# Cross-attention, first batch: another share-out of work between VectorE, ScalarE and GpSimd ahead of and in the first softmax

## The chip, the core and the metric

The kernel runs on one core of one Trainium2 chip. The metric is device time in microseconds for one execution; lower is better. TensorE (PE) multiplies matrices, VectorE (DVE), ScalarE (ACT) and GpSimd (POOL) do elementwise work, and SyncE (SP) issues the DMAs. The engines run their own instruction streams and wait for each other on semaphores. Each stream is in order: an instruction that waits holds back all that stand behind it.

## What is computed

Two layers on `x` [8, 512, 512]. The change touches only the first, a cross-attention with a gate:

```python
def _L0_xattn_ref(encoder_hc, decoder_hq, w_sim, b_sim, W_qv, b_qv):
    w1, w2, w3 = (w_sim[:d], w_sim[d:2 * d], w_sim[2 * d:])
    Sim = (encoder_hc @ w1)[:, :, None] + (decoder_hq @ w2)[:, None, :] \
        + jnp.einsum('bid,bjd->bij', encoder_hc * w3, decoder_hq) + b_sim[0]
    A = jax.nn.softmax(Sim, axis=2)
    hq_hat = jnp.einsum('bij,bjd->bid', A, decoder_hq)
    Batt = jax.nn.softmax(jnp.max(Sim, axis=2), axis=1)
    hc_bar = jnp.einsum('bi,bid->bd', Batt, encoder_hc)[:, None, :]
    hc_hat = jnp.broadcast_to(hc_bar, encoder_hc.shape)
    feats = jnp.concatenate([encoder_hc, hq_hat, encoder_hc * hq_hat, encoder_hc * hc_hat], axis=-1)
    return feats @ W_qv + b_qv

x = x + jnp.tanh(g_xattn[0]) * _L0_xattn_ref(_layernorm(x, axis=-1), ctx_1024, ...)
x = x + jnp.tanh(g_ffn[0]) * _L0_ffn_ref(_layernorm(x, axis=-1), ...)   # expert attention, unchanged
```

`encoder_hc` is the normalised `x` of a batch (512 rows of 512), `decoder_hq` its context.

## The kernel before

All is float32. To multiply at fp32 accuracy, each operand is kept as a pair: the upper part, which ScalarE makes by a copy into fp32r, and the lower part, operand less upper part, which VectorE or GpSimd makes (`take_lo`, L229 of both engines). Each product takes three passes over such pairs, so a 128 x 512 result over 512 inner rows is 12 matmuls.

The cross-attention runs over 8 batches. A batch is 4 tiles of 128 rows, and what is transposed is 4 tiles of 128 columns. For each batch:

- front: VectorE normalises `x` (`stage`; statistics L526, then the inverse square root by Newton steps in `mean_rstd`, L46 to L70, 17 small operations, then L537), TensorE turns it (L800), ScalarE copies it into `e_t` (L407). VectorE takes the dot of every row with `w1` (`row_dot`, L545, into `ew1`, then `+ b_sim`, L568) and makes `es_t` (scaled `e_t`, L557, and its lower part). ScalarE and VectorE or GpSimd split the transposed context `c_t` and the context `c`.
- softmax, one tile of 128 rows after another: 12 matmuls into `ps_s`, row maximum on VectorE (L594), `exp` on ScalarE (L435, with its sum), reciprocal and division on VectorE (L599, L601), turn on TensorE (L822), upper part on ScalarE (L440), lower part on VectorE (L606).
- attended: 4 x 12 matmuls into `ps_h` with the small softmax over rows between them (`ps_b`; `mtot` L613, `pmax` L617, `gmax` L677), `h_t` and `eh_t` as pairs (GpSimd makes the lower part of `eh_t`), and the weight block `wec = w_e + hc * w_c` as a pair (L715, L481, L229).
- features: 36 matmuls for each tile into `ps_f` with the weights `wh`, `weh`, `wec`; then the residual (L729), for which GpSimd has added the bias row to `x_sb` (L381). TensorE turns the next batch's rows between them, and has the last features of one batch between the scores of the next.

The loop over batches 1 to 7 is the same code for all; batch 0 has an order of its own written out (`first_front`, `first_softmax`, the head of GpSimd's stream), since the weights arrive and are split then too. Buffers are shared at the start: `x_sb` holds the first transposed context until batch 0's residual is loaded into it; `weh_raw` and `wh_raw` (in `spare`) hold the first context and a weight block, then the other blocks. SP's queue loads in order, each load waiting until its buffer is free: batch 1's `x` (L268, waits for the turn and the dot of each tile), the residual (L292), `weh_raw` behind `c_lo`, `we_raw` behind four `w_lo`, `wc_raw` behind eight.

In batch 0, TensorE turns batch 1's four tiles among the features, and these two waits tie that to GpSimd. ScalarE (L479 to L487), in `attended`:

```python
for k in range(ND):
    act.wait_ge(wec_ready, b * ND + k + 1)
    act.activation(wec[:, 0, k, :], tmp[:, k, :], ACT.Copy).then_inc(wec_hi, 1)
    if more and k in (1, 2):
        if k == 1:
            act.wait_ge(hc_ready, b * ND + ND)
            act.wait_ge(et_lo, b * ND + ND)
        copy_e(b + 1, k - 1)
```

and TensorE (L796 to L798), in `turn_e`: from the third tile on it waits for ScalarE's copy of the tile two before.

```python
if t >= 2:
    pe.wait_ge(et_copied, b * NT + t - 1)
```

## Time and profile before

| | us |
|---|---|
| median of 3 runs | 1286.59 |
| lowest and highest | 1286.2 and 1287.35 |
| the profiled execution | 1285.23 |
| its span from first to last instruction | 1283.4 |

| engine | busy us | share of the span |
|---|---|---|
| TensorE | 1216.2 | 95% |
| VectorE | 846.1 | 66% |
| GpSimd | 668.5 | 52% |
| ScalarE | 644.2 | 50% |

The granted clock of TensorE was 0.983 of full on average. Read first whose busy share is near the whole, then where in time that engine stands and for whom. The profile has views for that: windows (busy time of each engine in a stretch), waits (who waited for whom), the timeline (instructions in order of time, neighbours of one kind merged) and a view by line or tile. In the timeline a row is: start in us, duration in us, engine, line, operation, output <- inputs, shape, count, and in brackets how long the engine had stood before and who released it. The durations of TensorE's matmuls overlap a little.

### The profile page before, as it was taken

To read this page: it belongs to the slowest core of one execution; us is meant where nothing else is said; L and a number is where in the kernel's file an instruction comes from. 1 tells how busy PE (TensorE), PEld (TensorE's weight loads), DVE (VectorE), ACT (ScalarE), POOL (GpSimd) and SP (SyncE) were. 2 spreads that over 40 slices of the span, in tenths; PEclk is the share of its full clock that TensorE was granted. 3 is DMA by queue.
4 is the path that set the end of the run, shared out by engine and by line. 5 is a ranking of instruction groups with operands and counts; after the bars stand their busy time and mean duration, and the time that the engine had idled before them with its cause. 6 is when DMAs were issued, how large, how long until landed. Compare 5 with 4: busy or idle time off the path is not lost.

```text
span 1283.4 us, 19763 instructions
## 1 busy us (share of the span) xinstructions
PE 1216.2 (95%) x6376; PEld 910.7 (71%) x6376; DVE 846.1 (66%) x1527; ACT 644.2 (50%) x1418; POOL 668.5 (52%) x487
## 2 busy tenths in 40 slices
PE   3799999999999999699999999999999999999995
PEld 2588888888888888576767667667767667677663
DVE  7777777777776846264675665675665755756655
ACT  3343434344343431366566566556556656665551
POOL 4543342424242433339397395595593692872972
PEclk9799999999999999799999999999999999999998
DMA  6231313141323213400002002001010010010010
GB/s 215 96 115 50 114 49 123 41 123 41 123 68 96 91 55 134 136 1 13 22 2 98 1 16 82 0 33 65 0 65 33 0 65 33 0 65 0 8 57 33
DMA packets 40714, 75.74 MB, mean 59 GB/s; under 512 B 3760, under 2 KB 4272, under 8 KB 40688
## 3 DMA queue, kind: packets, MB, share of 16 engines
q1 hardware_dynamic: 40688, 75.42, 17.8%
q8 instruction: 13, 0.21, 0.1%
q14 instruction: 13, 0.11, 0.0%
HBM read 58.63 MB, written 16.78 MB: 59 GB/s over the span
## 4 chain that ended last, share of the span: by engine, by line
PE 48%; DVE 5%; POOL 3%; ACT 1%; issue 1%; DVEq 0%; POOLq 0%; ACTq 0%
PE ps_r L1651 11%; PE ps_o L1724 8%; PE ps_s L1711 8%; PE ps_s L1703 7%; PE ps_r L1663 5%; PE ps_r L1686 5%; DVE z L1438 2%; POOL v_acc L1243 2%; DVE z_tmp L1427 1%; POOL spare L1237 1%; PE ps_r L1677 1%; PE ps_r L1670 1%; PE ps_r L1640 1%; DVE nmax L1407 1%; DVE q L1465 0%
## 5 line engine op out<-in xcount | busy, mean ns | idle before, releaser
L1255 POOL TENSOR_TENSOR z<-z,z_tmp 128x1280 f32<-128x1280 f32 x40 | 117.2, 2929 | 199.6 <-DVE z_tmp L1427 197.5
L1407 DVE TENSOR_REDUCE nmax<-ps_s 128x1 f32<-128x512 f32 x256 | 163.6, 680 | 85.7 <-PE ps_s L1703 84.6
L1303 ACT ACTIVATE pt<-ps_s 128x512 f32<-128x512 f32 x256 | 139.2, 595 | 144.5 <-PE ps_s L1711 144.2
L1294 ACT ACTIVATE probs<-ps_s,nmax 128x512 f32<-128x512 f32 x256 | 174.3, 694 | 16.0 <-DVE nmax L1407 15.9
L1243 POOL TENSOR_TENSOR v_acc<-v_acc,spare 128x512 f32<-128x512 f32 x128 | 172.7, 1349 | 10.0
L1237 POOL TENSOR_TENSOR spare<-xv,pick 128x512 f32<-128x512 f32 x128 | 142.5, 1113 | 10.0
L1711 PEld LDWEIGHTS ps_s<-ident,probs 128*128 128x128 f32 x1024 | 109.5, 141 | 48.7 <-issue 40.8
L1711 PE MATMUL ps_s<-ident,probs 128*128 128x128 f32 x1024 | 140.3, 280 | 1.3 <-ACT probs L1294 1.2
L1703 PE MATMUL ps_s<-k,q 64*128 64x512 f32 x768 | 123.6, 426 | 3.7 <-ACT pt L1303 3.7
L1724 PE MATMUL ps_o<-pt,v_acc 128*64 128x512 f32 x512 | 116.9, 598 | 0.7 <-ACT pt L1303 0.7
L229 POOL TENSOR_TENSOR e_t<-e_t 128x512 fp32r<-128x512 f32 x32 | 40.7, 1311 | 146.9 <-ACT e_t L428 146.9
L1703 PEld LDWEIGHTS ps_s<-k,q 64*128 64x128 f32 x768 | 62.3, 184 | 55.8 <-issue 47.3
L788 PE MATMUL ps_h<-es_t,c 128*128 128x512 f32 x384 | 99.0, 408 | 0.0
L788 PE MATMUL ps_s<-c_t,es_t 128*128 128x512 f32 x384 | 96.2, 404 | 2.7 <-DVE es_t L229 2.7
L229 POOL TENSOR_TENSOR c<-stage,c 128x512 fp32r<-128x512 f32 x28 | 42.4, 1545 | 107.3 <-ACT c L225 107.3
L1651 PE MATMUL ps_r<-y_t,wq 128*128 128x512 f32 x384 | 97.7, 400 | 0.0
L1651 PE MATMUL ps_r<-y_t,wk 128*128 128x512 f32 x384 | 96.3, 396 | 0.0
L788 PE MATMUL ps_f<-weh,eh_t 128*128 128x512 f32 x384 | 94.8, 396 | 0.0
L788 PE MATMUL ps_f<-wh,h_t 128*128 128x512 f32 x384 | 93.1, 392 | 0.0
L788 PE MATMUL ps_f<-wec,e_t 128*128 128x512 f32 x384 | 91.9, 391 | 0.4 <-DVE wec L229 0.4
L1663 PE MATMUL ps_r<-wx,y_t 128*128 128x400 f32 x384 | 81.1, 362 | 6.8 <-DVE y_t L1461 4.3
L788 PEld LDWEIGHTS ps_s<-c_t,es_t 128*128 128x128 f32 x384 | 72.9, 194 | 18.2 <-DVE es_t L229 3.3
(169 smaller groups left out, 2160.5 us busy)
## 6 DMA issues: line engine op xcount, KB each, us to landing
stage<-in_x SPq DMA_DIRECT2D x32, 256.0 KB, 3.0
x_sb<-in_x SPq DMA_DIRECT2D x8, 1024.0 KB, 5.3
x_dram<-x_sb SPq DMA_DIRECT2D x32, 256.0 KB, 2.0
stage<-x_dram SPq DMA_DIRECT2D x8, 1024.0 KB, 5.6
spare<-x_dram SPq DMA_DIRECT2D x8, 1024.0 KB, 5.6
out_dram<-spare SPq DMA_DIRECT2D x32, 256.0 KB, 2.0
stage<-in_ctx_t SPq DMA_DIRECT2D x28, 256.0 KB, 3.4
stage<-in_ctx SPq DMA_DIRECT2D x28, 256.0 KB, 2.6
```

Of the source, the lines that this page charges most:

```text
L788: last = pe.matmul(out, left(l, k), right(r, k), start=start and n == 1, stop=stop and n == ND * len(PASSES))
L1237: pool.tensor_tensor(v_tmp[:] if e else acc, xv[:, :, e, :].unsqueeze(2).broadcast_to(shape), pick[:, 0, e, :, 2 * p:2 * p + 2].unsqueeze( ...
L1243: pool.tensor_tensor(acc, acc, v_tmp[:], ALU.add).then_inc(v_steps, 1)
L1255: pool.tensor_tensor(zv, zv, z_tmp[:, h % 2], ALU.add).then_inc(z_pool, 1)
L1294: act.activation(probs[:, n % BANKS, :], ps_s[:, n % BANKS, :], ACT.Exp, bias=nmax[:, n:n + 1], accum_out=den[:, h, t:t + 1]).then_inc(p_e ...
L1303: act.activation(pt[:, h % 4, :, t * P:(t + 1) * P], ps_s[:, n % BANKS, :].rearrange("p (k t) -> p k t", k=NT), ACT.Copy).then_inc(pt_read ...
L1407: dve.tensor_reduce(nmax[:, n:n + 1], ps_s[:, n % BANKS, :], AX_X, ALU.max, negate=True).then_inc(nmax_ready, 1)
L1651: end = pe.matmul(ps, w2[:, l, k, n * P:(n + 1) * P], y_t2[:, r, k, :], start=m == 0, stop=m == len(every) - 1)
L1663: end = pe.matmul(ps[:, 0:NX], y_t2[:, l, k, n * P:(n + 1) * P], wx2[:, r, k, :], start=m == 0, stop=m == len(every) - 1)
L1703: end = pe.matmul(ps_s[:, (n + a) % BANKS, :], q2[head_rows(a), p % 2, l, t * P:(t + 1) * P], k2[head_rows(a), p % 2, r, :], start=m == 0, ...
L1711: end = pe.transpose(ps_s[:, n % BANKS, k * P:(k + 1) * P], probs[:, n % BANKS, k * P:(k + 1) * P], ident[:])
L1724: end = pe.matmul(ps_o[head_rows(a), :], v_acc[:, p, k, a, :], pt[:, p % 2 * 2 + a, k, :], start=k == 0, stop=k == NT - 1)
```

## The change

Only batch 0 and GpSimd's share in it are changed:

- The lower parts of the first `c_t` go from GpSimd to VectorE: two ahead of `front`, two between the parts of `es_t`.
- GpSimd waits for `ew1_biased` (all four dots and the bias sum) before its first `c` part, and for the end of batch 1's Newton steps (`newton`) before the third `wh` part. Its later order is: `weh`, `eh_t`, `e_t`, three bias additions, then batch 1's `c`. Before, `e_t` stood ahead of `weh`, and each bias addition between two parts of `eh_t`.
- The division in the first softmax and the scaling of `bias_row` by the gate go from VectorE to ScalarE, where the copy of each turned tile also moves behind the following casts.
- All four dots of batch 0 move behind `es_t`: the first ahead of the first maximum, three behind it. Their products go into `x_sb`, no longer into `a_sb`, so the load of the residual into `x_sb` waits for `ew1_biased`.
- VectorE's order in the first softmax is another: statistics, maxima and the Newton steps of batch 1 are put elsewhere.

```diff
@@ sync
             load_x(1, second=True)
             sp.wait_ge(ct_lo, ND)
+            sp.wait_ge(ew1_biased, 1)
             load_residual(0)
@@ gpsimd
+            def scaled_lo(b, k):
+                pool.wait_ge(eh_hi, b * ND + k + 1)
+                take_lo(pool, eh_t2, k, tmp).then_inc(eh_lo, 1)
...
+            pool.wait_ge(ew1_biased, 1)
+            ctx_lo(0, True)
+            weight_lo(wh, wh_raw, 0, (0, 1))
+            pool.wait_ge(newton, 2 * ROOT_STEPS)
+            weight_lo(wh, wh_raw, 0, (2, 3))
+            weight_lo(weh, weh_raw, ND, range(ND))
             for k in range(ND):
-                pool.wait_ge(ct_hi, k + 1)
-                take_lo(pool, c_t2, k, x_sb).then_inc(ct_lo, 1)
-            ctx_lo(0, True)
-            weight_lo(wh, wh_raw, 0)
+                scaled_lo(0, k)
             rows_lo(0)
-            weight_lo(weh, weh_raw, ND)
-            with pool.Fori(0, B - 1) as b:
-                rest(b)
-                ctx_lo(b + 1)
-                add_bias(b, NT - 1)
-                rows_lo(b + 1)
+            add_bias(0, 0)
+            add_bias(0, 1)
+            add_bias(0, 2)
+            ctx_lo(1)
+            add_bias(0, NT - 1)
+            rows_lo(1)
+            with pool.Fori(0, B - 2) as b:
+                rest(b + 1)
+                ctx_lo(b + 2)
+                add_bias(b + 1, NT - 1)
+                rows_lo(b + 2)
@@ scalar
+            def normalise(b, t):
+                act.wait_ge(rden_ready, b * NT + t + 1)
+                act.activation(a_sb[:, t % 2, :], a_sb[:, t % 2, :], ACT.Copy, scale=rden[:, t:t + 1]).then_inc(a_ready, 1)
+
             def first_softmax():
                 softmax_exp(0, 0)
+                normalise(0, 0)
                 weights_hi(wh, wh_raw, wh_loaded, (0, 1))
+                probs_hi(0, 0)
                 softmax_exp(0, 1)
-                probs_hi(0, 0)
+                normalise(0, 1)
                 weights_hi(wh, wh_raw, wh_loaded, (2, 3))
+                probs_hi(0, 1)
...
@@ scalar, first_front
                 act.activation(gate[:], gate_raw[:], ACT.Tanh).then_inc(gate_ready, 1)
+                act.wait_ge(gate_ready, 1)
+                act.activation(bias_row[:], bias_row[:], ACT.Copy, scale=gate[:, 0:1]).then_inc(bias_ready, 1)
                 ctx_hi(0, True)
@@ vector, front
                     if not first:
-                        ctx_t_lo(b, k)
+                        ctx_t_lo(b, k, False)
+                    elif k < 2:
+                        ctx_t_lo(b, k + 2, True)
                     scaled_e_lo(b, k)
...
-                if first:
-                    row_dots(b, 2)
-                else:
+                if not first:
@@ vector, first_softmax
+                row_dot(0, 0, x_sb)
                 row_max(0, 0)
-                row_stats(1, 0)
-                normalise(0, 0)
+                row_dot(0, 1, x_sb)
+                invert(0, 0)
+                row_dot(0, 2, x_sb)
+                row_dot(0, 3, x_sb)
+                bias_dots(0)
                 row_max(0, 1)
-                row_stats(1, 1)
                 probs_lo(0, 0)
-                normalise(0, 1)
-                row_stats(1, 2)
-                row_stats(1, 3)
+                invert(0, 1)
+                row_stats(1, 0)
                 row_max(0, 2)
...
-                for part in range(4):
+                row_totals(0)
+                for part in range(5):
                     root(1, part)
...
@@ vector, start
+            for k in range(2):
+                ctx_t_lo(0, k, True)
+            front(0, True)
             dve.wait_ge(dots_loaded, 2 * 16)
-            for t in range(2):
-                row_dot(0, t)
-            front(0, True)
-            dve.wait_ge(gate_ready, 1)
-            dve.tensor_scalar(bias_row[:], bias_row[:], gate[:, 0:1], None, ALU.mult).then_inc(bias_ready, 1)
             first_softmax()
```

GpSimd's stream, from its first lower part through batch 0. In the names, `spare` is `weh_raw` or `wh_raw`, and `tmp` the scaled operand. Before:

```order
L229 TENSOR_TENSOR c_t<-x_sb,c_t 128x512 [waits ct_hi] x4
L229 TENSOR_TENSOR c<-spare,c 128x512 [waits c_hi] x4
L229 TENSOR_TENSOR wh<-spare,wh 128x512 [waits w_hi] x4
L229 TENSOR_TENSOR e_t<-e_t 128x512 [waits et_hi] x4
L229 TENSOR_TENSOR weh<-spare,weh 128x512 [waits w_hi] x4
L390 UNCONDITIONAL_BRANCH
L390 ISA
L229 TENSOR_TENSOR eh_t<-tmp,eh_t 128x512 [waits eh_hi]
```

GpSimd's stream at the same place after the change:

```order
L229 TENSOR_TENSOR c<-spare,c 128x512 [waits c_hi,ew1_biased]
L229 TENSOR_TENSOR c<-spare,c 128x512 [waits c_hi] x3
L229 TENSOR_TENSOR wh<-spare,wh 128x512 [waits w_hi] x2
L229 TENSOR_TENSOR wh<-spare,wh 128x512 [waits w_hi,newton]
L229 TENSOR_TENSOR wh<-spare,wh 128x512 [waits w_hi]
L229 TENSOR_TENSOR weh<-spare,weh 128x512 [waits w_hi] x4
L229 TENSOR_TENSOR eh_t<-tmp,eh_t 128x512 [waits eh_hi] x4
L229 TENSOR_TENSOR e_t<-e_t 128x512 [waits et_hi] x4
L385 TENSOR_TENSOR x_sb<-x_sb,bias_row 128x512 [waits res_loaded,bias_ready]
L385 TENSOR_TENSOR x_sb<-x_sb,bias_row 128x512 x2
```

The four `c_t` rows are gone, `e_t` has gone behind `weh` and all of `eh_t`, the additions stand behind that, and two waits for VectorE have come in.

VectorE's stream from the last two `es_t` parts into the first softmax (ISA rows are the dots with their sums). Before:

```order
L229 TENSOR_TENSOR es_t<-tmp,es_t 128x512 [waits es_hi] x2
L545 ISA a_sb,ew<-stage,w_row 128x512 [waits ew1_ready,e_ready]
L545 ISA ew 128x1
L545 ISA a_sb,ew<-stage,w_row 128x512 [waits ew1_ready,e_ready]
L545 ISA ew 128x1
L568 TENSOR_SCALAR ew<-ew,bsim_col 128x4 [waits ew1_ready]
L752 TENSOR_SCALAR bias_row<-bias_row,gate 128x512 [waits gate_ready]
L594 TENSOR_REDUCE nmax<-ps_s 128x1 [waits s_ready]
L526 BN_STATS stats<-stage 128x6 [waits slot_loaded0]
L599 RECIPROCAL rden<-den 128x1 [waits a_exp]
L601 TENSOR_SCALAR a_sb<-a_sb,rden 128x512 [waits rden_ready]
```

VectorE's stream at the same place after the change:

```order
L229 TENSOR_TENSOR es_t<-tmp,es_t 128x512 [waits es_hi] x2
L568 ISA x_sb,ew<-stage,w_row 128x512 [waits e_ready,dots_loaded]
L568 ISA ew 128x1
L620 TENSOR_REDUCE nmax<-ps_s 128x1 [waits s_ready]
L568 ISA x_sb,ew<-stage,w_row 128x512 [waits e_ready]
L568 ISA ew 128x1
L625 RECIPROCAL rden<-den 128x1 [waits a_exp]
L568 ISA x_sb,ew<-stage,w_row 128x512 [waits ew1_ready,e_ready]
L568 ISA ew 128x1
L568 ISA x_sb,ew<-stage,w_row 128x512 [waits ew1_ready,e_ready]
L568 ISA ew 128x1
L594 TENSOR_SCALAR ew<-ew,bsim_col 128x4 [waits ew1_ready]
```

One dot stands ahead of the first maximum (`nmax`) instead of two dots, the bias sum and the scaling of `bias_row`; the division of `a_sb` is gone, and the sum is now the last of this group.

## Rows read from the trace of the kernel before

**Rows 1.** Page, part 1: engine, busy us, share of the span, instructions.

```profile
PE 1216.2 (95%) x6376; PEld 910.7 (71%) x6376; DVE 846.1 (66%) x1527; ACT 644.2 (50%) x1418; POOL 668.5 (52%) x487
```

**Rows 2.** Windows: stretch, length, busy of each engine, then TensorE's clock, DMA.

```profile
29.00:49.00 20.00, 9.97 (x40) 7.48 (x40) 15.41 (x30) 9.96 (x22) 11.89 (x10) 0.74 0.42 154
```

**Rows 3.** Waits, to 80 us, then 60 to 560: us in total, times, longest.

```profile
PE ps_t L822 <- DVE a_sb L601: 9.1, 3, 5.3
...
PE ps_f L788 <- DVE wec L229: 0.4, 1, 0.4
```

**Rows 4.** Timeline at the first square root: GpSimd and VectorE.

```profile
8.08 4.94 POOL L229 TENSOR_TENSOR c_t<-x_sb,c_t 128x512 fp32r<-128x512 f32 x4 [6.44 <-ACT c_t L225]
...
8.21 1.17 DVE L58 TENSOR_SCALAR work<-work 128x4 int32<-128x4 int32 x1
...
13.07 0.16 DVE L70 SCALAR_TENSOR_TENSOR rstd<-work,rstd 128x4 f32<-128x4 f32 x1
13.26 0.16 DVE L66 TENSOR_TENSOR work<-rstd 128x4 f32<-128x4 f32 x1
```

**Rows 5.** Timeline, VectorE: the last two parts of `es_t`.

```profile
22.66 1.47 DVE L229 TENSOR_TENSOR es_t<-tmp,es_t 128x512 fp32r<-128x512 f32 x2
```

**Rows 6.** Timeline from the casts of `c` to the first `exp`.

```profile
23.41 2.18 ACT L225 ACTIVATE c<-spare 128x512 fp32r<-128x512 f32 x4
...
24.10 6.14 POOL L229 TENSOR_TENSOR c<-spare,c 128x512 fp32r<-128x512 f32 x4 [11.09 <-ACT c L225]
...
27.53 1.59 DVE L752 TENSOR_SCALAR bias_row<-bias_row,gate 128x512 f32<-128x512 f32 x1
29.05 0.68 DVE L594 TENSOR_REDUCE nmax<-ps_s 128x1 f32<-128x512 f32 x1
...
29.76 0.69 ACT L435 ACTIVATE a_sb<-ps_s,nmax 128x512 f32<-128x512 f32 x1 [4.17 <-DVE nmax L594]
```

**Rows 7.** By line (division: ns min/median/max, first and last start), then timeline.

```profile
L601 DVE TENSOR_SCALAR a_sb<-a_sb,rden x4: 486/1316/1339, 30.8 to 45.2; 128x512 f32<-128x512 f32 x4
...
43.15 0.69 ACT L435 ACTIVATE a_sb<-ps_s,nmax 128x512 f32<-128x512 f32 x1 [3.70 <-DVE nmax L594]
...
44.30 1.15 ACT L428 ACTIVATE e_t<-e_t 128x512 fp32r<-128x512 f32 x2
...
46.48 1.22 DVE L613 SCALAR_TENSOR_TENSOR mtot<-nmax,ew 128x4 f32<-128x4 f32 x1
```

**Rows 8.** Timeline, TensorE: the first blocks of `ps_h` and `ps_f`.

```profile
49.40 4.35 PE L788 MATMUL ps_h<-es_t,c 128*128 128x512 f32 x12
55.39 0.38 PE L843 MATMUL ps_b<-gmax,ones 1*128 1x1 f32 x2 [1.64 <-DVE gmax L677]
55.70 4.60 PE L788 MATMUL ps_h<-es_t,c 128*128 128x512 f32 x12
...
66.75 2.88 PE L788 MATMUL ps_f<-wh,h_t 128*128 128x512 f32 x12
```

**Rows 9.** Timeline where batch 1 is turned, all engines.

```profile
69.61 1.29 POOL L229 TENSOR_TENSOR eh_t<-tmp,eh_t 128x512 fp32r<-128x512 f32 x1 [1.11 <-ACT eh_t L478]
...
74.12 0.58 ACT L407 ACTIVATE e_t<-ps_t 128x512 f32<-128x512 f32 x1
...
75.90 0.60 PE L800 MATMUL ps_t<-ident,stage 128*128 128x128 f32 x4
76.12 1.47 DVE L229 TENSOR_TENSOR wec<-tmp,wec 128x512 fp32r<-128x512 f32 x2
...
79.55 5.60 PE L788 MATMUL ps_f<-wec,e_t 128*128 128x512 f32 x24
```

**Rows 10.** Timeline, GpSimd and VectorE at batch 1's `c`.

```profile
87.08 2.30 POOL L229 TENSOR_TENSOR c<-stage,c 128x512 fp32r<-128x512 f32 x1 [14.74 <-ACT c L225]
87.54 0.68 DVE L229 TENSOR_TENSOR es_t<-tmp,es_t 128x512 fp32r<-128x512 f32 x1
```

**Rows 11.** DMA from 26 to 40 us: KB each, median us to landing.

```profile
spare<-in_w_qv SPq DMA_DIRECT2D x2, 1024.0 KB, 5.4
```

More of the change, by code:

```diff
@@ L358, in ctx_lo, with weight_lo @@
                     take_lo(pool, c_2, t, weh_raw if first else stage).then_inc(c_lo, 1)
-            def weight_lo(pair, raw, before):
-                for k in range(ND):
+            def weight_lo(pair, raw, before, tiles):
+                for k in tiles:
                     pool.wait_ge(w_hi, before + k + 1)
@@ L368, in rows_lo @@
                     take_lo(pool, e_t2, k, e_t).then_inc(et_lo, 1)
+            def scaled_lo(b, k):
+                pool.wait_ge(eh_hi, b * ND + k + 1)
+                take_lo(pool, eh_t2, k, tmp).then_inc(eh_lo, 1)
             def rest(b):
                 for k in range(ND):
-                    pool.wait_ge(eh_hi, b * ND + k + 1)
-                    take_lo(pool, eh_t2, k, tmp).then_inc(eh_lo, 1)
+                    scaled_lo(b, k)
                     if k:
@@ L538, in normalise_x, with row_dot @@
                                   ALU.subtract, ALU.mult).then_inc(e_ready, 1)
-            def row_dot(b, t):
+            def row_dot(b, t, products=junk):
                 dve.wait_ge(e_ready, b * NT + t + 1)
@@ L544, in row_dot, with ctx_t_lo @@
                     dve.wait_ge(ew1_ready, b * NT + t - 1)
-                dve.tensor_tensor_reduce(out=junk[:, t % 2, :], in0=e_sb[:, t, :], in1=w1_row[:], scale=1.0,
+                dve.tensor_tensor_reduce(out=products[:, t % 2, :], in0=e_sb[:, t, :], in1=w1_row[:], scale=1.0,
                                          scalar=0.0, op0=ALU.mult, op1=ALU.add,
                                          accum_out=ew1[:, t:t + 1]).then_inc(ew1_ready, 1)
-            def ctx_t_lo(b, k):
+            def ctx_t_lo(b, k, first):
                 dve.wait_ge(ct_hi, b * ND + k + 1)
-                take_lo(dve, c_t2, k, stage).then_inc(ct_lo, 1)
+                take_lo(dve, c_t2, k, x_sb if first else stage).then_inc(ct_lo, 1)
             def scaled_e(b, k, first):
@@ L562, in scaled_e_lo, with row_dots, bias_dots @@
                 take_lo(dve, es_t2, k, tmp).then_inc(es_lo, 1)
-            def row_dots(b, begin=0):
-                for t in range(begin, NT):
+            def row_dots(b):
+                for t in range(NT):
                     row_dot(b, t)
+                bias_dots(b)
+            def bias_dots(b):
                 dve.wait_ge(ew1_ready, b * NT + NT)
@@ L595, in row_max, with invert, normalise @@
                     nmax_ready, 1)
-            def normalise(b, t):
+            def invert(b, t):
                 dve.wait_ge(a_exp, b * NT + t + 1)
                 dve.reciprocal(rden[:, t:t + 1], den[:, t:t + 1]).then_inc(rden_ready, 1)
+            def normalise(b, t):
+                invert(b, t)
                 dve.wait_ge(rden_ready, b * NT + t + 1)
@@ L619, in first_softmax @@
             def first_softmax():
+                row_dot(0, 0, x_sb)
                 row_max(0, 0)
+                row_dot(0, 1, x_sb)
[3 more added lines that the diff above has]
+                bias_dots(0)
+                row_max(0, 1)
+                probs_lo(0, 0)
+                invert(0, 1)
                 row_stats(1, 0)
-                normalise(0, 0)
-                row_max(0, 1)
+                row_max(0, 2)
                 row_stats(1, 1)
-                probs_lo(0, 0)
-                normalise(0, 1)
+                probs_lo(0, 1)
+                invert(0, 2)
                 row_stats(1, 2)
+                row_max(0, 3)
                 row_stats(1, 3)
-                row_max(0, 2)
-                probs_lo(0, 1)
-                normalise(0, 2)
-                for part in range(4):
+                probs_lo(0, 2)
+                invert(0, 3)
+                row_totals(0)
+                for part in range(5):
                     root(1, part)
-                row_max(0, 3)
-                probs_lo(0, 2)
-                normalise(0, 3)
-                row_totals(0)
                 probs_lo(0, 3)
                 row_totals_max(0)
-                for part in range(4, ROOT_PARTS):
+                for part in range(5, ROOT_PARTS):
                     root(1, part)
```

5 lines of the change are left out of this document (3 added, 2 removed).

## Prediction

> **What bounds the kernel now.** I read the page's busy shares first: TensorE is busy 95% of the span [rows 1], so only time that TensorE loses can be won. The windows by stage say where it loses: from 29 to 49 us it works 9.97 of 20 us, at a mean granted clock of 0.74 [rows 2], part of it at the lower of its two levels (1.2 instead of 2.4 GHz). The waits of TensorE up to 80 us name one releaser above all, VectorE's division of `a_sb` (9.1 us in three waits), and from 60 to 560 us there is just 0.4 us behind a wait in cross-attention [rows 3]. So batch 0's front, up to about 57 us, is a chain of waits, and behind it TensorE sets the pace: what comes off the front comes off the end, and every new wait of TensorE behind it is added.
>
> What stretches the front is in the timeline. The small VectorE operations of the square root take 0.16 us each and follow every 0.20 us once GpSimd is idle, but the four from 8.21 us take 1.17 to 1.19 us, while GpSimd works on `c_t` from 8.08 to 13.02 us [rows 4]. They end one by one with GpSimd's operations (1.24 us each). The same shows at the division of `a_sb`: shortest 0.486 us, median 1.316 us [rows 7], the short one the only one that GpSimd left alone. Operations that read PSUM are not held: the maximum at 29.05 us takes 0.68 us beside GpSimd's fourth `c` part [rows 6]. The two engines take turns where VectorE reads SBUF twice or runs at its double rate.
>
> **The change, part by part.** All on the profiled execution's own time, 1285.23 us (span 1283.4 and 1.8 around it); the median of the three runs is 1286.59, 1.36 above.
>
> (1) *The lower parts of `c_t` go from GpSimd to VectorE.* The operation at 13.07 would start 0.20 us after each of four, at 9.01: 4.06 us earlier. The four operations now on VectorE: two fall in its wait for `e_t` (it has no dot products to do there any more), two fall between the parts of `es_t`, at 0.61 us each. ScalarE's copy of the next part hides part of them, so the last part of `es_t`, which ended at 24.13 [rows 5], ends at 20.98 instead of 20.07. **-3.15 us** here.
>
> (2) *Dot products 2 and 3, the bias sum and the scaling of `bias_row` leave the place before the first maximum.* Before: two dots and the sum, then the scaling at 27.53 with 1.59 us, and only then the maximum at 29.05 and `exp` at 29.76 [rows 6], 5.63 us behind `es_t`. Now three things must be over: one dot (0.7) and the maximum (0.7); TensorE's first block of scores; and ScalarE, which gets one more 0.63 us operation ahead of the four `c` casts (2.18 us [rows 6]). ScalarE: the last `es_t` cast ends 20.26, gate and bias row 21.0, casts 23.2. TensorE: its last three matmuls start at 21.0 and end near 22.6, so the maximum ends at 23.3. `exp` starts at 23.33, 2.35 us behind `es_t`. **-3.28 us**; 6.4 so far.
>
> (3) *The first softmax, four row blocks.* Division on ScalarE costs 0.63 us against 0.49 and saves the 0.8 us by which it was held three times. Placing the operations forward, a block now costs ScalarE: from the start of `exp` over its sum and VectorE's reciprocal to the division 1.0 (29.76 to 30.8, rows 6 and 7), division 0.55 (start to start), two casts 1.15, copy of the turned block 0.5 (43.15 to 44.30, less the 0.69 of `exp`): 3.2 us [rows 7]. TensorE needs 3.3 for 12 matmuls and a turn, about the same. The four `exp` start at 23.3, 26.9, 30.3 and 33.5, where before the first and last were 13.39 us apart (29.76, 43.15). Behind the last: division at 34.5, two casts 1.15, copy 0.6, lower part 0.7, the reduction to `pmax`: TensorE's first `ps_h` matmul at 38.0. Before it was at 49.40, 6.25 behind the last `exp` (the division held, and `mtot` behind it with 1.22 us [rows 7]). From the first `exp` to `ps_h`: 14.7 against 19.64, **-4.95 us**.
>
> (4) *`ps_h`.* Before, VectorE's square root for batch 1 was held again by GpSimd's work on `weh`, so the maximum of `ps_b` came late: TensorE stood for 1.64 us, and the 12 matmuls behind the gap took 4.60 us at the low clock [rows 8] against 2.8 for 12 at full (24 take 5.60 [rows 9]). GpSimd now waits for the end of that square root (`newton`), so nothing holds it: it ends at 39.5, in the shadow of the first `ps_h` block, which I leave at the 4.35 us of [rows 8]. The gap goes, and with it the low clock behind it: **-3.1 us**. The first `ps_f` matmul then stands at 52.3, before 66.75: **14.5 us earlier in all**.
>
> *What GpSimd is now late for.* It starts when the bias sum is done (26.0), so `c` is finished at 31.1; nobody needs it before 38.0. The load of `weh_raw` is queued on SP behind `c_lo` and behind the new wait for `ew1_biased`, lands 5.4 us later [rows 11] at 36.5, and its casts come at 36.9. `wh` waits for the square root and ends at 42.0, `weh` at 47.6, then `eh_t`; `ps_f` wants them from 52.3 and 59 on. The last raw load, queued behind `w_lo`, lands at 53; it is wanted at 56.5. All hidden, the closest with 3 us. The wait of the residual load costs nothing: it is wanted far later.
>
> (5) *`rows_lo(0)` and three bias additions now stand behind all of `eh_t`.* This is the term against the change. I stay in the times of before (subtract 14.5). GpSimd ends its last `eh_t` at 70.9 [rows 9]. Before, one addition followed; now four parts of `e_t` do, then the additions. In the same place VectorE has eight operations that read SBUF twice (the `wec` sums and lower parts, 5.2 us of work), and ScalarE's copy of the turned batch 1 into `e_t`, at 74.12 [rows 9], waits for `et_lo` of all four; the third and fourth `wec` casts stand behind that copy, and TensorE's third turn (`ps_t` at 75.90) waits for it. Taking turns: `e_t` part 0 to 72.3, two VectorE operations to 73.6, part 1 to 74.8, four to 77.3, part 2 to 78.5, part 3 to 79.75. The copy ends at 80.4, the second copy (behind one cast) at 81.4, so TensorE begins its fourth turn at 81.5 and the next block at 81.85 where it was 76.69: **+5.1 us**. The last part of `wec` is done at 83.5, before TensorE asks for it (84.7), where before it asked at 79.55 and `wec` had ended at 77.6.
>
> How VectorE and GpSimd share that stretch has two answers in the trace: at 24.10, with four `c` parts in 6.14 us between VectorE's dots and sums [rows 6], they take strict turns; at 87.08 GpSimd waits through two VectorE operations (2.30 us; VectorE's second one began at 87.54, after GpSimd had asked) [rows 10]. The above goes by the second. With strict turns the `e_t` parts end at 77.8, but `wec` only at 84.55, and TensorE waits there: +5.0 us. The bounds: all twelve port operations without additions between would end `wec` at 81.2 (+1.9); all three additions ahead of the last one, with TensorE waiting twice, +6.
>
> The Trainium skill (SBUF — State Buffer, "Who interferes with whom") says that a VectorE instruction with two SBUF inputs, or in a 2-port mode, and a GpSimd instruction lock each other out for a whole instruction, and that issue order decides who blocks. This case's rows of 1.17 us against 0.16 agree with the lock [rows 4]; the 2.30 us row at 87.08 does not agree with issue order [rows 10]. By the rule as it stands the sum would take +5.0 here instead of +5.1.
>
> (6) *The clock.* TensorE stands for 4.7 us at that turn. After a gap of 1.64 us the trace shows the low clock and 4.60 us for 12 matmuls [rows 8]; I take the same loss here, **+1.6 us**, with 0 and 3.5 (two such stretches) as ends.
>
> **Sum:** -14.5 + 5.1 + 1.6 = -7.8 us: profiled execution 1277.4, median 1286.59 - 7.8 = **1278.8 us** (-0.6%). The gain lies between 12 (TensorE at the low clock through the first two score blocks, or the first `ps_h` block wholly low) and 16; the give-back between 1.9 and 9.5. So the likeliest case alone is 1274.7 to 1284.
>
> **The rivals.** *A: nothing is given back.* GpSimd gets its four `e_t` parts through in time. That gives 1286.59 - 14.5 = 1272.1. For it: `et_lo` may come at 75.9 if GpSimd wins every turn. Against: then VectorE's eight operations end late instead, and TensorE waits for `wec`. Chance 0.07.
>
> *B: about no change.* The low clock holds through both first score blocks (the mean of 0.74 from 29 to 49 us shows such stretches [rows 2]) and again behind the turn: gain 11.2, give-back 9: 1284.4. Softmax blocks would show TensorE late instead of ScalarE. Chance 0.09.
>
> *C: slower, since the long VectorE operations are not GpSimd's doing.* Then the change does not do what it says: of the gain, 4.06 in (1), 2.5 in the divisions, 1.1 at `mtot` and 3.1 in (4) fail, 3.7 us stay, and the later copies still cost 6.7: 1289.6. It decides once less than 6.7 us of the gain comes. The operations' ends fall on GpSimd's, so 0.03.
>
> *D: slower by the clock.* The 4.7 us gap before batch 1's third turn leaves the clock low. Work at half rate costs its own length again, so from 9.4 us of such work the gain is gone, from 12 us on the kernel is slower by 0.2%; through all the 22 us up to batch 1's softmax it would be 1299. [...] Chance 0.03.
>
> **Chances and range.** Forecast 0.78, A 0.07, B 0.09, C 0.03, D 0.03. About 0.2% (2.6 us) is what a measurement can tell from no change: faster 0.87, same 0.08, slower 0.05. The range takes the forecast's bounds and reaches half-way towards A and to the edge of B: 1273.5 to 1284.0.
>
> **What would show it.** (1) The square root's operations 0.16 us each, `ps_t` turns from 11.0; (2) first `exp` near 23.3, ScalarE without a long wait ahead; (3) `exp` every 3.3 us, first `ps_h` at 38; (4) no TensorE gap between the first two `ps_h` blocks, first `ps_f` near 52.3; (5) GpSimd's `e_t` parts behind `eh_t`, a ScalarE wait for GpSimd before `e_t`, a TensorE wait of 4 to 5 us before the third turn of batch 1; (6) clock under 1 behind it. From about 75 us on every row should stand some 7.8 us earlier. I am wrong if TensorE waits in the softmax for ScalarE's casts longer than placed, if `et_lo` comes before the copy is due, or if the raw loads come late.

## The result, and the profile after

The changed kernel took 1277.2 us in the median of four runs (1277.08 to 1278.41), the kernel before 1286.49 (1286.2 to 1287.35) beside it. The ratio is 0.9929, with a 95% interval of 0.9912 to 0.9946: 9.3 us faster, where 7.8 were forecast. The profiled execution took 1278.41 us, its span is 1276.6, and the mean granted clock 0.984, so between the two profiled executions there are 6.8 us.

The page's busy shares of the changed kernel say nothing yet: TensorE is busy 95% of the span, as in [rows 1], of a shorter span. The windows do tell something. Their columns are those of [rows 2]. The first row is the front: TensorE works 16.08 of 20 us, where it worked 9.97; this window, which starts 7 us earlier, now takes in the first `ps_h` block too (5.19 us). The second is the stretch from the first `ps_f` block with `weh` to batch 1's scores. It is 22.29 us long; the same work took 17.39 before (73.04 to 90.43). The last two lie at the end of the kernel.

```profile
22.00:42.00 20.00, 16.08 (x68) 12.25 (x66) 12.88 (x43) 14.91 (x31) 11.36 (x10) 0.83 0.53 160
57.89:80.18 22.29, 18.33 (x84) 14.18 (x82) 21.78 (x31) 10.26 (x19) 11.70 (x7) 1.00 0.29 86
1245.00:1255.00 10.00, 6.31 (x24) 1.97 (x21) 6.46 (x5) 1.49 (x3) 5.78 (x2) 0.83 0.00 0
1255.00:1265.00 10.00, 4.68 (x17) 3.96 (x18) 5.68 (x6) 1.79 (x3) 0.00 (x0) 0.58 0.01 2
```

The timeline of the changed kernel, all engines, from the square root to batch 1's scores, and the last two blocks of the kernel:

```profile
7.85 0.17 DVE L61 TENSOR_SCALAR rstd<-work 128x4 int32<-128x4 int32 x1
...
9.62 0.16 DVE L70 SCALAR_TENSOR_TENSOR rstd<-work,rstd 128x4 f32<-128x4 f32 x1
...
19.21 1.47 DVE L229 TENSOR_TENSOR es_t<-tmp,es_t 128x512 fp32r<-128x512 f32 x2
...
22.95 0.69 ACT L448 ACTIVATE a_sb<-ps_s,nmax 128x512 f32<-128x512 f32 x1
...
36.50 0.37 PE L871 MATMUL ps_b<-ident,pmax 128*1 128x128 f32 x1 [1.56 <-DVE pmax L646]
36.70 5.19 PE L820 MATMUL ps_h<-es_t,c 128*128 128x512 f32 x12
...
42.13 3.02 PE L820 MATMUL ps_h<-es_t,c 128*128 128x512 f32 x12
...
51.60 2.89 PE L820 MATMUL ps_f<-wh,h_t 128*128 128x512 f32 x12
...
55.72 6.54 POOL L229 TENSOR_TENSOR e_t<-e_t 128x512 fp32r<-128x512 f32 x4
55.96 3.47 DVE L749 SCALAR_TENSOR_TENSOR tmp<-spare,hc 128x512 f32<-128x512 f32 x2
...
59.35 1.78 DVE L229 TENSOR_TENSOR wec<-tmp,wec 128x512 fp32r<-128x512 f32 x1
...
62.34 0.60 ACT L420 ACTIVATE e_t<-ps_t 128x512 f32<-128x512 f32 x1 [2.24 <-POOL e_t L229]
63.08 0.63 PE L832 MATMUL ps_t<-ident,stage 128*128 128x128 f32 x4 [2.17 <-ACT e_t L420]
...
64.48 2.98 PE L820 MATMUL ps_f<-weh,eh_t 128*128 128x512 f32 x12
...
68.54 5.73 PE L820 MATMUL ps_f<-wec,e_t 128*128 128x512 f32 x24 [1.07 <-DVE wec L229]
...
77.92 2.30 POOL L229 TENSOR_TENSOR c<-stage,c 128x512 fp32r<-128x512 f32 x1 [10.59 <-ACT c L225]
...
80.18 5.60 PE L820 MATMUL ps_s<-c_t,es_t 128*128 128x512 f32 x24
...
1246.02 5.35 PE L1756 MATMUL ps_o<-pt,v_acc 128*64 128x512 f32 x16 [0.69 <-ACT pt L1335]
...
1263.11 10.29 PE L1718 MATMUL ps_r<-wo,z_t 128*128 128x512 f32 x36 [1.46 <-DVE z_t L1505]
```

Read it against the rows of before. The operation on `rstd` that stood at 13.07 [rows 4] stands at 9.62, and all are 0.16 to 0.17 us long. The first `exp` has gone from 29.76 [rows 6] to 22.95, the first `ps_h` matmul from 49.40 to 36.70, the first `ps_f` from 66.75 to 51.60 [rows 8], and the gap in `ps_h` is gone. At 55.96 two VectorE operations take 3.47 us beside GpSimd's `e_t`: strict turns. There ScalarE waits for GpSimd, TensorE for ScalarE (2.17 us, `ps_t`), and TensorE once more for `wec` (1.07 us). Batch 1's scores begin at 80.18, before at 90.43: 10.25 us earlier.

Those 10.25 us are still there near the end. The same two last blocks of the kernel before, in its timeline:

```profile
1256.23 3.65 PE L1724 MATMUL ps_o<-pt,v_acc 128*64 128x512 f32 x16 [0.69 <-ACT pt L1303]
...
1271.62 8.61 PE L1686 MATMUL ps_r<-wo,z_t 128*128 128x512 f32 x36 [1.46 <-DVE z_t L1473]
```

1256.23 - 1246.02 = 10.21 us. Then the same 16 matmuls take 5.35 us in place of 3.65 and the same 36 take 10.29 in place of 8.61, at a granted clock of 0.83 and 0.58 in those windows: 3.4 us lost in the last 30, in code that the change leaves alone. That is the whole difference between the 10.2 us up to there and the 6.8 us of the two profiled executions. The medians differ by 9.3 since the profiled execution of the changed kernel lies 1.2 us above its median, and that of the kernel before (1285.23) 1.3 us below.

### The profile page after: what moved, and what is told of

It reads as the page before. It is cut to its first block, busy times and chain, and to the rows that moved or that the text cites. A ratio compares the mean times of both kernels' runs of the same rounds, so it can differ in the third digit from the quotient of the medians.

```text
span 1276.6 us, 19756 instructions
## 1 busy us (share of the span) xinstructions
PE 1217.5 (95%) x6376; PEld 909.8 (71%) x6376; DVE 837.4 (66%) x1526; ACT 647.6 (51%) x1423; POOL 664.8 (52%) x483
## 4 chain that ended last, share of the span: by engine, by line
PE 48%; DVE 5%; POOL 3%; issue 1%; ACT 1%; DVEq 0%; POOLq 0%; ACTq 0%
PE ps_r L1683 11%; PE ps_o L1756 9%; PE ps_s L1743 8%; PE ps_s L1735 7%; PE ps_r L1695 5%; PE ps_r L1718 5%; DVE z L1470 2%; POOL v_acc L1275 2%; POOL spare L1269 1%; DVE z_tmp L1459 1%; PE ps_r L1709 1%; PE ps_r L1702 1%; PE ps_r L1672 1%; DVE nmax L1439 1%; DVE q L1497 0%
```

## The experiments

Unless told otherwise an experiment is the changed kernel with one edit. Times are medians, with the ratio to the kernel before on the same chip and its 95% interval.

### The changed kernel once more

> The changed kernel, unaltered, beside the improved one on the same chip and against the same runs of before. Both theories: about 1277 us, 0.992 to 0.994 of before. What it tells apart is how much of the spread lies outside the first batch: if the last two long blocks of TensorE (16 matmuls of ps_o, 36 of ps_r) again show 5.35 and 10.3 us, the tail is tied to this kernel's timing; if they show 3.65 or 8.6, it changes from run to run.

No edit. Measured 1277.17 us (1275.61 to 1279.76), 0.9933 [0.9919, 0.9946]. The timeline of its TensorE:

```profile
64.13 0.63 PE L832 MATMUL ps_t<-ident,stage 128*128 128x128 f32 x4 [2.17 <-ACT e_t L420]
...
69.60 5.74 PE L820 MATMUL ps_f<-wec,e_t 128*128 128x512 f32 x24 [1.08 <-DVE wec L229]
...
1264.36 10.37 PE L1718 MATMUL ps_r<-wo,z_t 128*128 128x512 f32 x36 [1.46 <-DVE z_t L1505]
```

The two waits come back to 0.01 us: they belong to the order of the work. The third turn of batch 1 is 1.05 us later (64.13 against 63.08). The loads of `x`, which landed later, are 0.42 of that (first turn at 10.93 against 10.51); most of the rest is that TensorE took longer over the same first scores and the first `ps_h` block (5.42 against 5.19). The five runs spread over 4.2 us. Nothing under about 1.5 us is therefore decided by the times alone.

Of the last two blocks the expectation asked whether they would be long again. They were, 5.35 and 10.37 us, which by its own test speaks for a tail tied to this kernel's timing. Two executions cannot rule out chance.

### Where the gain comes from

**`c_t` back on GpSimd.**

```diff
+            for k in range(ND):
+                pool.wait_ge(ct_hi, k + 1)
+                take_lo(pool, c_t2, k, x_sb).then_inc(ct_lo, 1)
             pool.wait_ge(ew1_biased, 1)
@@ vector
-                    elif k < 2:
-                        ctx_t_lo(b, k + 2, True)
...
-            for k in range(2):
-                ctx_t_lo(0, k, True)
             front(0, True)
...
+            dve.wait_ge(ct_lo, ND)
             first_softmax()
```

> The changed kernel with its first part undone: the four lower parts of c_t are GpSimd's again, ahead of its wait for ew1_biased. Theory (lock): four operations of the first square root take 1.2 us each again (+4.06), VectorE is rid of four operations (-0.9): +3.2, about 1280.4 us. Rival (ScalarE or the loads set the first exp): less than 1.5 us slower.

Measured 1281.03 us, 0.996 [0.9947, 0.9972]: 3.8 us slower than the changed kernel. Its timeline:

```profile
7.86 4.93 POOL L229 TENSOR_TENSOR c_t<-x_sb,c_t 128x512 fp32r<-128x512 f32 x4 [6.23 <-ACT c_t L225]
...
9.18 1.19 DVE L61 TENSOR_SCALAR rstd<-work 128x4 int32<-128x4 int32 x1
...
14.91 1.09 PE L832 MATMUL ps_t<-ident,stage 128*128 128x128 f32 x4 [14.91 <-DVE stage L563]
...
68.67 4.33 PE L820 MATMUL ps_f<-weh,eh_t 128*128 128x512 f32 x12
72.84 5.61 PE L820 MATMUL ps_f<-wec,e_t 128*128 128x512 f32 x24
```

The long operations of the square root are back (1.16 to 1.19 us, four of them, as in [rows 4]) and the first turn is 4.4 us later than after the change (10.51). This is the largest single part. Rival C, that the length of VectorE's operations has nothing to do with GpSimd, is out by this alone: the same operation takes 1.19 us with GpSimd at work and 0.17 without. The last two rows belong to the clock, below.

**GpSimd without its wait for the Newton steps.**

```diff
             weight_lo(wh, wh_raw, 0, (0, 1))
-            pool.wait_ge(newton, 2 * ROOT_STEPS)
             weight_lo(wh, wh_raw, 0, (2, 3))
```

> The changed kernel without GpSimd's wait for batch 1's square root. Theory (lock): weh follows its casts from 36.7 us and holds four of VectorE's small operations, the maximum of ps_b comes near 42.4 instead of 38.0, TensorE (which needs it at 41.8) stands for about 0.6 us: +0.6, with a low clock behind the gap +2. So 1277.8 to 1279.5. Rival (the first ps_h block hides it all): 1277.2 with no gap.

Measured 1278.76 us, 0.9949 [0.9933, 0.9966]: 1.5 us slower. Its timeline:

```profile
36.66 5.00 POOL L229 TENSOR_TENSOR weh<-spare,weh 128x512 fp32r<-128x512 f32 x4 [1.21 <-ACT weh L225]
...
37.99 1.21 DVE L68 SCALAR_TENSOR_TENSOR work<-work 128x4 f32<-128x4 f32 x1
...
42.59 0.27 DVE L710 TENSOR_REDUCE gmax<-ps_b 1x1 f32<-1x128 f32 x1
42.91 0.38 PE L874 MATMUL ps_b<-gmax,ones 1*128 1x1 f32 x2 [0.69 <-DVE gmax L710]
...
65.93 4.25 PE L819 MATMUL ps_f<-weh,eh_t 128*128 128x512 f32 x12
```

`weh` holds four of the small operations (0.88 to 1.21 us), `gmax` comes at 42.59 where it was at 38.02 after the change, and TensorE gets a gap of 0.69 us between the `ps_h` blocks; before it was 1.64 [rows 8]. The wait on GpSimd removes that gap, as the prediction's step (4) says. It also keeps `wh` off `mtot` and the start of the square root (1.05 and 1.32 us long here), which the prediction did not count: TensorE stands for 2.33 us ahead of the first `ps_b`, and for 1.56 after the change. The gap and the longer wait are the edit's. What they cost in the whole stands at the edge of what the runs can tell: the first `ps_f` block comes at 52.70, after the change at 51.60 and in `changed_again` at 52.66, and this trace lost another 1.2 us near 600 us, in code that the edit leaves alone.

**Division on VectorE.**

```diff
@@ scalar, after each of the four exp
-                normalise(0, t)
@@ vector
-                invert(0, t)
+                normalise(0, t)
```

> The changed kernel with the four divisions of the first softmax on VectorE again. Theory (lock): GpSimd works on c and wh from 25.5 to 33.1 us, so the second and third division take 1.3 instead of 0.49 us and TensorE stands behind them. The first is free (-0.2). About +1 us by the first ps_h block, 1278 to 1279. Rival (ScalarE's own order is what costs): ScalarE, rid of four operations of 0.72 us, is done earlier, and the run is 0 to 1 us faster.

Measured 1278.68 us, 0.9958 [0.9944, 0.9972]: 1.5 us slower. Its timeline:

```profile
27.46 1.27 DVE L626 TENSOR_SCALAR a_sb<-a_sb,rden 128x512 f32<-128x512 f32 x1
...
65.60 4.59 PE L816 MATMUL ps_f<-weh,eh_t 128*128 128x512 f32 x12
```

Two of four divisions meet GpSimd (1.27 and 1.44 us), two do not (0.49 each). From the first `exp` to `ps_h` it takes 15.64 us in place of 13.75. The division on ScalarE takes 0.72 us (four times 721 to 726 ns), more than the 0.49 of a free VectorE, and still wins 1.9 us, since it is never held there. The rival, that ScalarE's order is what costs, is out for this stretch: rid of the four operations, the way to `ps_h` got longer.

**All dots ahead of the first maximum.**

```diff
+                for t in range(NT):
+                    row_dot(0, t, x_sb)
+                bias_dots(0)
-                row_dot(0, 0, x_sb)
                 row_max(0, 0)
```

> The changed kernel with all four dots and the bias sum ahead of the first maximum. Theory (VectorE is the last of three there): the maximum, now at 22.2 us, starts at 22.8, when the dots end 2.2 us later than one does: first exp at 23.5 to 23.7 instead of 22.95, and the rest keeps that, +0.6: 1277.8. Rival (more than VectorE): the first exp 2 us late, 1279.

Measured 1278.1 us, 0.9945 [0.9928, 0.9961]. Its timeline:

```profile
25.57 0.69 ACT L448 ACTIVATE a_sb<-ps_s,nmax 128x512 f32<-128x512 f32 x1 [1.14 <-DVE nmax L620]
```

From the scores (18.77) to the `exp` it is 6.80 us, where it is 5.72 after the change (17.23 to 22.95): 1.08 us, for three dots and the sum. It is less than their work, since VectorE stood for 0.93 us there after the change, waiting for TensorE's scores. The time differs by 0.9 us, within what the runs scatter, and the profiled execution's start was 1.5 us late besides. Of the four parts undone one at a time this moved the median least.

### What is given back

**Only the later rows, on the kernel before.** Part (5) of the change alone:

```diff
             weight_lo(wh, wh_raw, 0)
-            rows_lo(0)
             weight_lo(weh, weh_raw, ND)
+            for k in range(ND):
+                pool.wait_ge(eh_hi, k + 1)
+                take_lo(pool, eh_t2, k, tmp).then_inc(eh_lo, 1)
+            rows_lo(0)
+            for t in range(NT - 1):
+                add_bias(0, t)
+            ctx_lo(1)
```

> The kernel before with one part of the change alone: GpSimd makes all eh_t parts, then the e_t parts, then the three bias additions. Theory (late rows): from the first ps_f block with weh to batch 1's scores 22.3 us instead of 17.4, a ScalarE wait for GpSimd ahead of the copy, +4.9 us, 1.3 more if the clock falls in the gap: 1290 to 1292. Something is given back to that: with e_t away from the softmax, GpSimd holds two divisions and the mtot operations less, -1 to -3. In all 1287 to 1291. Rival (rows are late only because GpSimd starts later in the changed kernel): within 1 us of before.

Measured 1288.03 us, 1.0019 [1.001, 1.0029]: 2.6 us slower than the 1285.47 of the kernel before, beside it. Its timeline:

```profile
46.62 4.73 PE L796 MATMUL ps_h<-es_t,c 128*128 128x512 f32 x12
...
66.51 6.53 POOL L229 TENSOR_TENSOR e_t<-e_t 128x512 fp32r<-128x512 f32 x4
...
73.12 0.60 ACT L415 ACTIVATE e_t<-ps_t 128x512 f32<-128x512 f32 x1 [2.24 <-POOL e_t L229]
...
75.62 3.94 PE L796 MATMUL ps_f<-weh,eh_t 128*128 128x512 f32 x12
...
90.94 5.60 PE L796 MATMUL ps_s<-c_t,es_t 128*128 128x512 f32 x24
```

The wait of 2.24 us and the 6.53 us of `e_t` are those of the changed kernel, and its stretch from 68.68 to 90.94 is 22.26 us long, where the changed one has 22.29 and the kernel before 17.39. So the give-back belongs to this one move, in the kernel before as in the changed one. What the move pays ahead: with `e_t` out of the softmax one division is held instead of three and `mtot` is free, and `ps_h` comes at 46.62 where it came at 49.40 [rows 8], 2.8 us earlier (0.3 of it by the loads of `x`). By the first `ps_f` block it is 4.4 us, so batch 1's scores start just 0.5 us later than before. The time lies in what was expected (1287 to 1291), but the 2.6 us of the medians are no measure of the give-back: in the profiled execution TensorE reached the last `ps_o` block 1.1 us earlier than before and lost 3.3 us in the two long blocks at the end.

**`e_t` back in GpSimd's wait.**

```diff
             weight_lo(wh, wh_raw, 0, (0, 1))
+            rows_lo(0)
             pool.wait_ge(newton, 2 * ROOT_STEPS)
...
-            rows_lo(0)
             add_bias(0, 0)
```

> The changed kernel, but GpSimd makes the four lower parts of e_t while it waits for VectorE's square root (idle from 33.07 to 38.17 us in the trace of the changed kernel), not behind eh_t. Theory (late rows): the give-back of 4.9 us comes from et_lo and from the turns at the port around it, so it goes nearly whole: about 1272.5 us, no ScalarE wait for GpSimd ahead of the copy of batch 1, no TensorE wait before its third turn. Rival (the port work only moves): the four parts hold the square root, and with it wh and the maximum of ps_b, by as much as they save: 1276 to 1278, with a TensorE gap between the first two ps_h blocks.

Measured 1277.28 us, 0.9933 [0.9911, 0.9956]: no difference. Its timeline:

```profile
34.66 4.94 POOL L229 TENSOR_TENSOR e_t<-e_t 128x512 fp32r<-128x512 f32 x4
35.86 1.31 DVE L46 TENSOR_TENSOR work<-stats 128x8 f32<-128x8 f32 x1
...
41.07 0.37 PE L871 MATMUL ps_b<-ident,pmax 128*1 128x128 f32 x1 [4.61 <-DVE pmax L646]
```

What the later stretch wins (it is 19.30 us long, 3.0 less), the softmax loses: `e_t` now falls on the square root of batch 1 and the way to `pmax`, and TensorE stands for 4.61 us ahead of `ps_b` where it stands for 1.56 after the change. GpSimd's idle time was no free place for its work, because VectorE was not idle in it.

**`e_t` ahead of `eh_t`.**

```diff
+            rows_lo(0)
             for k in range(ND):
                 scaled_lo(0, k)
-            rows_lo(0)
             add_bias(0, 0)
```

> The changed kernel, but GpSimd makes the four e_t parts between weh and eh_t, from 45.8 us. Theory (late rows): eh_t ends near 56 where it ended at 55.7, which nobody waits for, so again about 1272.5 us. Rival (late eh_t): the first eh_t parts come at 52 to 56 instead of from 47, VectorE's wec sums, which wait for them, and TensorE's ps_f with weh are late: 1275 to 1278.

Measured 1276.4 us, 0.9926 [0.9908, 0.9945]. Its timeline:

```profile
62.27 0.63 PE L832 MATMUL ps_t<-ident,stage 128*128 128x128 f32 x4 [0.20 <-ACT e_t L420]
...
64.64 0.63 PE L832 MATMUL ps_s<-ident,stage 128*128 128x128 f32 x4 [1.74 <-ACT e_t L420]
...
78.72 5.60 PE L820 MATMUL ps_s<-c_t,es_t 128*128 128x512 f32 x24
```

The wait ahead of the third turn falls from 2.17 to 0.20 us and the one for `wec` is gone, but another of 1.74 comes at the fourth turn: the bias additions now take turns with the `wec` operations. The stretch (59.06 to 78.72) is 19.66 us long, so 2.6 of the 4.9 us come back in the trace; the median moves by 0.8, within the scatter.

**`e_t` ahead, additions apart.** Two placings, which came out lowest of all:

```diff
+            rows_lo(0)
             for k in range(ND):
                 scaled_lo(0, k)
-            rows_lo(0)
-            add_bias(0, 0)
-            add_bias(0, 1)
+                if k in (1, 2):
+                    add_bias(0, k - 1)
+            pool.wait_ge(wec_lo, ND)
             add_bias(0, 2)
```

> The changed kernel with GpSimd's e_t parts between weh and eh_t, bias additions 0 and 1 behind the second and third eh_t part as before the change, and addition 2 only when wec is finished. Theory (the rest of the give-back is additions at the port): with e_t moved alone, TensorE still stood 0.2 and 1.7 us at the turns, and 19.66 us passed from the first ps_f block with weh to batch 1's scores, against 17.39 before the change and 22.29 after it. Without the additions there it should be 17.4 to 17.7 again, some 2 us faster than that run: 1274 to 1275. Rival (the eight VectorE operations and ScalarE's copies are the chain, whoever else is at the port): still 19.5.

```diff
+            rows_lo(0)
             for k in range(ND):
                 scaled_lo(0, k)
-            rows_lo(0)
+            pool.wait_ge(wec_lo, ND)
             add_bias(0, 0)
             add_bias(0, 1)
             add_bias(0, 2)
```

> As the run with e_t parts and additions moved, but all three bias additions wait until wec is finished. There the last eh_t part ended only at 60.1 us, held by addition 1 and by VectorE's wec sums, and TensorE still stood 0.26 and 0.64 us at the turns. Theory (every port operation ahead of the turns costs its time): eh_t ends near 57, before the wec sums, from the first ps_f block with weh to batch 1's scores 17.4 to 17.7 us instead of 18.65, about 1 us faster than that run, 1273. Rival (the additions now hold batch 1's dot products and es_t instead): as much is lost again before batch 1's scores.

Measured 1274.04 us, 0.991 [0.9894, 0.9927], and 1273.64 (1271.31 to 1275.91), 0.9909 [0.9895, 0.9923]. The timeline of the first of them:

```profile
63.20 0.63 PE L833 MATMUL ps_s<-ident,stage 128*128 128x128 f32 x4 [0.64 <-ACT e_t L421]
...
77.30 5.60 PE L821 MATMUL ps_s<-c_t,es_t 128*128 128x512 f32 x24
```

And of the second:

```profile
62.23 0.60 PE L833 MATMUL ps_t<-ident,stage 128*128 128x128 f32 x4
63.78 1.77 DVE L569 CUSTOM_DVE_ANT_0 a_sb<-stage,w_row 128x512 f32<-128x512 f32 x1
...
72.05 3.01 PE L821 MATMUL ps_f<-wh,h_t 128*128 128x512 f32 x12 [0.59 <-DVE x_sb L764]
77.62 5.60 PE L821 MATMUL ps_s<-c_t,es_t 128*128 128x512 f32 x24
...
597.57 2.43 PE L1696 MATMUL ps_r<-wx,y_t 128*128 128x400 f32 x12 [2.59 <-ACT logits L1362]
```

With all additions behind `wec` no turn of TensorE waits at all; in their place three of batch 1's four dots are held (1.77 us each), and TensorE waits 0.59 us for VectorE's `x_sb`. The stretches are 18.65 and 18.25 us: 3.6 and 4.0 of the 4.9 us come back, and 3.2 to 3.5 in the medians. Neither reached the 17.4 to 17.7 that was expected: what the additions no longer hold at the turns they hold at the dots, as the rival of the second run has it, in part. Which of the two is better the runs do not tell.

### The landmarks of all traces

To tell what an edit did from what moved by itself, each profiled execution is cut at three landmarks in TensorE's rows: its first turn, batch 1's scores, and the last `ps_o` block. All in us:

| kernel | first turn at | from there to batch 1's scores | from there to the last `ps_o` block | from there to the end |
|---|---|---|---|---|
| before | 15.14 | 75.29 | 1165.80 | 27.2 |
| after | 10.51 | 69.67 | 1165.84 | 30.6 |
| `changed_again` | 10.93 | 70.47 | 1165.87 | 30.6 |
| `ct_on_gpsimd` | 14.91 | 69.23 | 1165.53 | 29.3 |
| `no_newton_wait` | 10.63 | 70.69 | 1167.05 | 28.5 |
| `division_on_vector` | 10.00 | 71.36 | 1165.82 | 29.3 |
| `dots_before_max` | 12.04 | 71.01 | 1165.99 | 27.3 |
| `late_rows_alone` | 14.79 | 76.15 | 1164.18 | 30.5 |
| `rows_in_wait` | 11.39 | 69.47 | 1164.08 | 30.7 |
| `rows_before_eh` | 10.90 | 67.82 | 1165.85 | 29.4 |
| `rows_and_adds_moved` | 11.19 | 66.11 | 1165.94 | 30.7 |
| `all_adds_last` | 11.15 | 66.47 | 1163.75 | 30.4 |

The edits touch only what lies in the first two columns. The third still ranges over 3.3 us. Most of that comes from one place in the second layer, where TensorE has waited some 2.6 us for ScalarE's `logits`: the same 12 matmuls of `ps_r` with `wx` took 2.43 us in `all_adds_last` (its last row above), 3.88 after the change and 4.34 in `no_newton_wait`. The fourth ranges over 3.5 us by the last two long blocks. So a difference of 2 or 3 us between two traces, or two medians, need not be the edit's. The second column is not free of it either: the same kernel shows 69.67 and 70.47.

## Why the prediction was right, and where it was not

The sign, the size and the mechanism of the gain held: -9.3 us against -7.8. That the number came so near is in part luck. In the profiled pair the forecast's terms add up to -10.25 us at batch 1's scores, and 3.4 us that no term stood for were lost at the end. By its steps:

(1) and (2), up to the first `exp`: forecast 6.4 us, measured 6.81 (29.76 to 22.95). `es_t` ended 3.45 us earlier (forecast 3.15), but 0.57 of that is no effect of the change: the load of `x` landed earlier, and the square root began at 6.82 in place of 7.39. So the step itself gave 2.88. The stretch behind `es_t` took 2.27 us (forecast 2.35).

(3) From the first `exp` to `ps_h`: forecast 14.7, measured 13.75. The `exp` came 3.15 us apart three times. That is the 3.2 us which the text had worked out for a block; its own times for the four `exp` stood 3.6, 3.4 and 3.2 apart, which is too far. The division on ScalarE is 0.72 us long, and 0.63 from its start to the next one's.

(4) From `ps_h` to `ps_f`: forecast 14.3, measured 14.90. The gap and the low clock behind it went. By the text's own rows they were 3.4 us (1.64, and 4.60 less 2.8), not 3.1. But the first block took 5.19 us where 4.35 had been taken over from [rows 8] (4.24 to 5.46 over the experiments). Together the first `ps_f` came 15.15 us earlier, where 14.5 were forecast.

(5) The give-back: forecast 5.1, measured 4.90 (22.29 - 17.39). The amount is right by luck, for the way to it was the other one. The text chose, of the two readings that the trace of before offered, the one in which GpSimd waits through two VectorE operations [rows 10]. The changed kernel shows strict turns here, of 1.74 to 1.78 us (VectorE's 3.47 for two, GpSimd's 6.54 for four). With the one reading TensorE would have stood for 4 to 5 us ahead of the third turn and never for `wec`; in fact it stood for 2.17 there, 0.39 at the fourth, and 1.07 for `wec`, as the discarded reading has it (+5.0). That reading is also what the prediction took from issue order, the rule of the Trainium skill (SBUF — State Buffer, "Who interferes with whom"), and this stretch agrees with it. The other kind of sharing is real too: in the changed kernel the first part of batch 1's `c`, asked for at 77.92, again takes 2.30 us, beside a VectorE operation that began at 77.77 and one that began at 78.37. Issue order does not explain that, and no run here shows what decides between the two.

(6) The clock: forecast +1.6, and it cost nothing, with the clock up or down. This is the term that was wrong. In the profiled execution the block behind the gap took 2.98 us, and 2.98 again in `changed_again` and 3.00 in `dots_before_max`. In `ct_on_gpsimd`, `no_newton_wait`, `division_on_vector` and `late_rows_alone` the same 12 matmuls took 4.33, 4.25, 4.59 and 3.94 us, so the low clock that the text feared does come. But there TensorE no longer stood for `wec` (the row at 72.84 in `ct_on_gpsimd` has no wait), and the stretch from the first `ps_f` block with `weh` to batch 1's scores was 22.33, 22.33, 22.35 and 22.26 us long, against 22.29, 22.45 and 22.17 with the fast block. `wec` was what TensorE needed last there, and a slow block only filled the time for which TensorE would have waited. The mistake follows from (5): in the chosen reading TensorE never waits for `wec`, so a slow block would have been added whole. When the low clock comes is not settled.

What the sum had no term for is the end of the kernel: 3.4 us in the profiled pair, over the last two long blocks. The text said that from 75 us on every row should stand 7.8 us earlier. The rows stood 10.25 earlier at batch 1's scores, 10.21 at the last `ps_o` block, and 6.8 at the end. Which of these differences the unprofiled executions had is not known, so the 1.5 us between forecast and medians cannot be shared out among the terms.

The likeliest case, too, was bounded too narrowly: with a gain of up to 16 and a give-back of at least 1.9 its own bounds reach down to 1272.5 us, not 1274.7. The result lies in it either way.

Of the rivals, A (nothing given back) is out by the waits of 2.17 and 1.07 us. B is out by the 15.15 us at the first `ps_f` block and the give-back of 4.90, where it had 11.2 and 9. D is out since the stretch was no longer with a slow block than with a fast one. C is out by `ct_on_gpsimd`.

How much is shown of the gain by parts: the four that were undone one at a time cost 3.8 (`c_t`), 1.5 (division), 1.5 (Newton wait) and 0.9 us (dots) in the medians, 7.7 in all, of which the last three are each near the scatter of the runs. They are parts of the 15.15 us at the first `ps_f` block and not of the net, since the give-back stays in each of these kernels. In `late_rows_alone`, moving `e_t` out of the softmax gave 4.4 us there, 0.3 of it by the loads. The rest, some 3 us by subtraction if the parts simply add, was not tried by itself: `bias_row` on ScalarE, GpSimd's wait for `ew1_biased`, and the new places of statistics, maxima and Newton steps.

## What to carry to other kernels

Where two engines take turns, as VectorE and GpSimd do in these traces, an operation costs its partner a whole operation, however small the partner's is: place long ones where the other engine reads PSUM, runs on something else or truly waits, and put the small operations of a chain where nobody holds them. An engine's idle time is a free place only if its partner is idle too (`rows_in_wait`), and work that is put off to make a front shorter comes due in the next stretch: ask for each moved operation who waits for it there, and where it meets the partner again. A slow block ahead of a wait that something else ends costs nothing: before a term for the clock is added, ask what ends the stretch. Read a stretch's length from landmarks in the trace, since the median of the whole carries the scatter of start, middle and end.

## What the runs showed of the hardware

- The small VectorE operations of the square root took 0.15 to 0.17 us alone and up to 1.32 (the first one, in `no_newton_wait`) while GpSimd was at work.
- The start moves by itself. With the same instructions ahead of it, the first turn of TensorE came between 10.00 and 12.04 us in nine profiled executions, as the loads of `x` landed; a microsecond or two of a whole time is this.
- The end varies too: 16 matmuls took 3.65 or 5.33 to 5.35 us, and 36 took 8.61 to 10.83 us, in unchanged code behind waits of up to 6 us, over all kernels here. Near 600 us the same 12 matmuls took 2.42 to 4.34 us behind a wait of some 2.6. Two executions of the changed kernel agreed (5.35 twice, 10.29 and 10.37; 3.88 and 3.76 near 600 us), so this may go with a kernel's timing or change by chance; in neither case is it work that an edit elsewhere has saved or added.
- A `Copy` with a scale for each partition on ScalarE took 0.72 us for 128 x 512 floats (the division and the scaling of `bias_row`) and the plain casts between them 0.61; from one start to the next it was 0.63 and about 0.52. VectorE's division took 0.49 alone and 1.27 to 1.44 beside GpSimd.
